# Six expert tiles moved into the end of the graph stage, and the first tile list made from the counts of 22 groups

## What is computed

```python
x = x + gnn(layernorm(x), adj, ...)        # agg = eps*x + adj @ x; silu(rmsnorm(agg @ W1 + b1)) @ W2 + b2
x = x + ffn(layernorm(x), ...)
# ffn:
topk_vals, topk_idx = top_k(x @ gate_w + gate_b, 2)
topk_w = softmax(topk_vals)
expert_out = relu(x @ w1[e] + b1[e]) @ w2[e] + b2[e]       # experts 16, hidden 256
y = x + sum(topk_w * expert_out at topk_idx)
out = (y - mean(y)) / sqrt(var(y) + 1e-5) * gamma + beta
```

## Time and profile before

| what | value |
|---|---|
| median of 3 runs | 845.04 us |
| the profiled execution's time | 846.69 us |
| its span, first to last instruction | 844.9 us |
| PE busy, weight loads | 737.2 us (87%), 570.2 us (67%) |
| DVE, ACT, POOL busy | 625.5, 528.4, 519.3 us |
| mean granted TensorE clock | 0.946 of full |

### The profile page before, as it was taken

One profiled execution on the slowest core, in us unless ns is written; L12 is line 12 of the kernel. 1 busy time (PEld: TensorE's weight loads), 2 busy tenths in 40 slices (PEclk: granted clock), 3 DMA queues, 4 the chain that ended last, 5 costly groups with the idle time before them and its releaser, 6 DMA issues. The chain is left out here.

```text
span 844.9 us, 18953 instructions
## 1 busy us (share of the span) xinstructions
PE 737.2 (87%) x4709; PEld 570.2 (67%) x4710; DVE 625.5 (74%) x2290; ACT 528.4 (63%) x1123; POOL 519.3 (61%) x540
## 2 busy tenths in 40 slices
PE   4899999999999999995289999999999999998700
PEld 3577777787787777874167777777777777776500
DVE  2589999999999998886657666567776776666664
ACT  2589999999999999985223333355545445444441
POOL 3004777776677777767540067767777773777774
PEclk9799999999999999998579999999999999999955
DMA  5365555555555553221465577778888887888632
GB/s 160 117 227 193 176 167 176 190 190 191 182 173 177 167 174 121 74 82 53 118 195 150 156 204 197 211 206 225 235 229 229 225 225 206 225 231 223 196 109 81
DMA packets 141531, 149.20 MB, mean 177 GB/s; under 512 B 18835, under 2 KB 113059, under 8 KB 141222
## 3 DMA queue, kind: packets, MB, share of 16 engines
q1 hardware_dynamic: 122614, 111.13, 43.5%
q0 software_dynamic: 16384, 34.11, 14.2%
q10 hardware_dynamic: 2480, 3.40, 1.3%
HBM read 83.02 MB, written 65.55 MB: 176 GB/s over the span
## 5 line engine op out<-in xcount | busy, mean ns | idle before, releaser
L482 POOL DMA_INDIRECT dispatched<-rows,slot_i x256 | 258.3, 1009 | 169.1 <-issue 160.7
L501 POOL DMA_INDIRECT work<-results,place x184 | 182.7, 993 | 118.7 <-DVE tout L1200 63.2
L817 ACT ACTIVATE hid<-bank,wts 128x256 f32<-128x256 f32 x286 | 119.9, 470 | 212.1 <-PE bank L681 210.2
L1200 DVE SCALAR_TENSOR_TENSOR tout<-bank,gate,tin 128x128 f32<-128x128 f32 x286 | 87.2, 346 | 119.3 <-PE bank L696 118.4
L696 PE MATMUL bank<-w_all,hid 128*128 x1144 | 165.9, 288 | 0.0
L681 PE MATMUL bank<-tut,wts 128*128 128x256 f32 x572 | 150.0, 386 | 6.9 <-DVE tut L1183 6.9
L696 PEld LDWEIGHTS bank<-w_all,hid 128*128 128x128 f32 x1144 | 138.7, 191 | 17.2 <-issue 0.2
L533 PEld LDWEIGHTS bank<-w_sb,work 128*128 128x128 f32 x1024 | 123.2, 194 | 17.6 <-issue 14.6
L533 PE MATMUL bank<-w_sb,work 128*128 128x128 f32 x1024 | 126.4, 278 | 1.6 <-ACT work L796 1.6
L527 PE MATMUL bank<-agg,w_sb 128*128 128x512 f32 x256 | 125.2, 612 | 0.0
L681 PEld LDWEIGHTS bank<-tut,wts 128*128 128x128 f32 x572 | 98.6, 193 | 16.4 <-DVE tut L1183 8.1
(11 more groups left out here) (186 smaller groups left out, 1049.3 us busy)
## 6 DMA issues: line engine op xcount, KB each, us to landing
tin<-dispatched SPq DMA_DIRECT2D x143, 132.0 KB
wts<-in_w_exp SPq DMA_DIRECT2D x143, 129.0 KB
results<-tout SPq DMA_DIRECT2D x26, 704.0 KB, 5.2
results<-tout SPq DMA_DIRECT2D x143, 128.0 KB
xs<-in_x SPq DMA_DIRECT2D x32, 256.0 KB, 3.3
adj_sb<-in_adj_t SPq DMA_DIRECT2D x32, 256.0 KB
rms_b<-r_row SPq DMA_DIRECT2D x32, 256.0 KB, 3.5
out<-agg SPq DMA_DIRECT2D x32, 256.0 KB
```

The source lines that it names most:

```text
L482: nc.gpsimd.indirect_dma_start(dispatched, bass.IndirectOffsetOnAxis(slot_i[:, k, n:n + 1], 0), rows[:, k, n // TOPK, n % TOPK, :], None). ...
L501: nc.gpsimd.indirect_dma_start(moe_of(g)[:, n // TOPK, n % TOPK, :], None, results, bass.IndirectOffsetOnAxis(place[:, g, n:n + 1], 0)).th ...
L817: last = nc.scalar.activation(hid[:, n % 2, c, :], hid_ps[n % 2][:, c * TILE:(c + 1) * TILE], ACT.Relu, bias=wts[:, k, F + c:F + c + 1], s ...
L1200: last = nc.vector.scalar_tensor_tensor(out=tout[:, k, a, :], in0=exp_ps[n % 2][:, a * D:(a + 1) * D], scalar=gate[:, n % 2, a:a + 1], in1 ...
```

## The change

The first six tiles (0 to 5) are no longer run behind the routing, but between its last steps, in an order that is written out by hand for PE, ACT and DVE: after step 32 come tile steps -1 and 0, after step 33 tile step 1, after step 34 tile step 2, and so on to tile step 5; the totals, the whole list and the pads go in between. For that their list has to exist earlier. It is now made from the counts of 22 groups (EARLY_AT), which PE sums in step 25 and DVE turns into the six entries in six parts, one at the end of each of steps 26 to 31. SyncE waits for the scatters of 22 groups instead of 29. The counts of all segments are still taken after step 31 (`tiles_by_then`, `lists_of_tiles`: the old block without the first list). FIRST is 10 (tiles behind it are loaded only when everything is scattered), which makes MIX_FROM 44. DVE's first wait for a stored tile moves from tile 3 to tile 6. Each engine's tile loop now starts behind tile step 5. SyncE's order of work is unchanged.

```diff
 RING2 = 6
 NT = TOK * TOPK // TILE + E - 1
 CAP_T = CAP // TILE
-FIRST = 9
+FIRST = 10
+EARLY_AT = 22
+EARLY_STEP = EARLY_AT + 3
 FULL_AT = 29
 SEGS = (2, 4, 6, 9, 12, 15, 18, 21, 25, FULL_AT)
...
-                sp.wait_ge(scattered[k], 16 * GB * TOPK * len(range(k, FULL_AT, RING)))
+                sp.wait_ge(scattered[k], 16 * GB * TOPK * len(range(k, EARLY_AT, RING)))
...
-            pipeline(eng, tile_step, -1, 7, NG // RING2, MIX_FROM, RING2)
+            pipeline(eng, tile_step, RING2, 2 * RING2 + 1, NG // RING2 - 1, MIX_FROM, RING2)
...
+                    if i is None and t == EARLY_STEP + 1:
+                        pe.wait_ge(early_out, 1)
...
+                if i is None and t == EARLY_STEP:
+                    pe.wait_ge(hist_done, EARLY_AT)
+                    for q, upto in enumerate((SEGS[0], EARLY_AT)):
+                        for j in range(GB):
+                            last = nc.tensor.matmul(q_ps[:, (4 + q) * E:(5 + q) * E], ones_b[:], hist[:, upto - 1, j, :],
+                                                    start=(j == 0), stop=(j == GB - 1))
+                    last.then_inc(early_done, 1)
...
-            pipeline(pe, step, *P1)
+            pipeline(pe, step, *P1[:3], NG)
...
+                    listed = first_table if i is None and n < RING2 else table
+                    e = pe.value_load(listed[0:1, bass.ds(count(i, n, 1, RING2), 1), 1], min_val=0,
...
+            step(None, NG)
             pe.wait_ge(x1_done, NG)
-            pe.wait_ge(table_done, 1)
+            pe.wait_ge(z_done, HC * NG)
+            pe.wait_ge(rb_out, NG)
+            pe.wait_ge(first_done, 1)
             pe.wait_ge(b2_in, 16)
             pe.wait_ge(w2_in, 16 * FC)
-            pipeline(pe, tile_step, *P2, RING2)
+            tile_step(None, -1)
+            tile_step(None, 0)
+            step(None, NG + 1)
+            tile_step(None, 1)
+            step(None, NG + 2)
+            tile_step(None, 2)
+            pe.wait_ge(carry_done, NG)
+            pe.wait_ge(slote_done, NG)
+            pe.wait_ge(ms_out, NG)
+            for j in range(GB):
+                last = nc.tensor.matmul(misc_ps[:, 0:E], ones_b[:], carry[:, NG % RING, j, :],
+                                        start=(j == 0), stop=(j == GB - 1))
+            last.then_inc(tot_done, 1)
+            tile_step(None, 3)
+            tile_step(None, 4)
+            pe.wait_ge(cols_done, 1)
+            for q in range(2):
+                nc.tensor.transpose(q_ps[0:1, q * (P + E):q * (P + E) + P], t_c[:, q, 0:1], ident[:])
+                last = nc.tensor.transpose(q_ps[0:1, q * (P + E) + P:(q + 1) * (P + E)], t_c[0:E, q, 1:2],
+                                           ident[0:E, 0:E])
+            last.then_inc(rows_done, 1)
+            pe.wait_ge(back_done, 1)
+            nc.tensor.transpose(misc_ps[0:1, 0:P], t_c[:, 2, 0:1], ident[:])
+            nc.tensor.transpose(misc_ps[0:1, P:P + E], t_c[0:E, 2, 1:2], ident[0:E, 0:E]).then_inc(rows_done, 1)
+            tile_step(None, 5)
+            pe.wait_ge(table_done, 1)
+            pipeline(pe, tile_step, RING2, P2[1], P2[2], P2[3], RING2)
...
-            pipeline(act, step, *P1)
+            pipeline(act, step, *P1[:3], NG)
...
+            step(None, NG)
+            tile_step(None, 0)
+            step(None, NG + 1)
+            tile_step(None, 1)
+            step(None, NG + 2)
+            for t in range(2, 5):
+                tile_step(None, t)
+            act.wait_ge(pad_done, 1)
+            _, starts = nc.values_load_multi_w_load_instructions(
+                pad_row[0:1, E // 2:E], engines=[mybir.EngineType.Activation], min_val=0, max_val=E * CAP)
+            for r in starts:
+                act.dma_start(pad_rows(r), pad[:]).then_inc(padded, 16)
+
+            tile_step(None, 5)
...
+            def early_tiles(part):
+                ceil, full = nt_ef[:, 0], nt_ef[:, 1]
+                if part == 0:
+                    link(nc.vector.tensor_scalar(nt_e[:, 0, 0], early_c[:, 0], float(TILE - 1), None, ALU.add))
+                    link(nc.vector.tensor_scalar(nt_e[:, 0, 1], early_c[:, 1], 0.0, None, ALU.add))
+                    link(nc.vector.tensor_single_scalar(nt_e[:, 1], nt_e[:, 0], TILE.bit_length() - 1,
+                                                        op=ALU.arith_shift_right))
+                    link(nc.vector.tensor_copy(nt_ef[:], nt_e[:, 1]))
+                if part == 1:
+                    link(nc.vector.tensor_tensor(pick[:, 0:E], full, ceil, ALU.min))
+                    link(nc.vector.tensor_tensor(pick[:, E:], full, pick[:, 0:E], ALU.subtract))
+                    link(nc.vector.tensor_copy(run2[:, 0, E:], pick[:]))
+                for step in {1: (0,), 2: (1, 2, 3, 4)}.get(part, ()):
+                    a, b = run2[:, step % 2], run2[:, (step + 1) % 2]
+                    link(nc.vector.tensor_tensor(b[:, E:], a[:, E:], a[:, E - (1 << step):3 * E - (1 << step)], ALU.add))
+                if part == 3:
+                    link(nc.vector.scalar_tensor_tensor(out=fill[:], in0=pick[:], scalar=float(FIRST),
+                                                        in1=run2[:, 1, E:], op0=ALU.add, op1=ALU.subtract))
+                    link(nc.vector.scalar_tensor_tensor(out=fill[:], in0=fill[:], scalar=0.0, in1=pick[:],
+                                                        op0=ALU.max, op1=ALU.min))
+                    link(nc.vector.tensor_tensor(upto_t[:, 1, :], fill[:, 0:E], fill[:, E:], ALU.add))
+                    link(nc.vector.tensor_copy(run[:, 0, NS - 1, E // 2:], upto_t[:, 1, :]))
+                if part == 4:
+                    running_sum(NS - 1, 1)
+                if part == 5:
+                    across = lambda a: a.unsqueeze(1).broadcast_to([1, RING2, E])
+                    link(nc.vector.tensor_scalar(away[:], upto_t[:, 1, :], -1.0, float(CAP_T), ALU.mult, ALU.add))
+                    link(nc.vector.tensor_tensor(f_m[:, 0], across(run[0:1, 0, NS - 1, E // 2:]),
+                                                 iota_ef[0:1, 0:RING2].unsqueeze(2).broadcast_to([1, RING2, E]),
+                                                 ALU.is_le))
+                    link(nc.vector.tensor_tensor(f_m[:, 1], f_m[:, 0], across(away[0:1, :]), ALU.mult))
+                    link(nc.vector.tensor_reduce(f_s[:], f_m[:], axis=AX.X, op=ALU.add))
+                    link(nc.vector.tensor_tensor(f_r[:], f_s[:, 1, :], iota_ef[0:1, 0:RING2], ALU.add))
+                    link(nc.vector.tensor_scalar(first_table[:, :, 0], f_r[:], float(TILE), None, ALU.mult))
+                    nc.vector.tensor_scalar(first_table[:, :, 1], f_s[:, 0, :], float(P), None, ALU.mult)\
+                        .then_inc(first_done, 1)
...
+                    if i is None and t == EARLY_STEP:
+                        dve.wait_ge(early_done, 1)
+                        nc.vector.tensor_copy(early_c[:], q_ps[:, 4 * E:6 * E].rearrange("p (q e) -> p q e", e=E))\
+                            .then_inc(early_out, 1)
-                if i is None and t == NG:
-                    first_tiles()
+                if i is None and EARLY_STEP < t < NG:
+                    early_tiles(t - EARLY_STEP - 1)
...
-                    if n >= LAG:
+                    if i is None and n == RING2:
+                        for k in range(RING2 - LAG):
+                            dve.wait_ge(t_kept[k], 16)
+                        k = n % RING2
+                    if n >= RING2:
...
-                if i is None and t == 0:
-                    late_tables()
...
+            step(None, NG)
+            tile_step(None, -1)
+            step(None, NG + 1)
+            tile_step(None, 0)
+            tiles_by_then()
+            tile_step(None, 1)
+            step(None, NG + 2)
+            tile_step(None, 2)
+            lists_of_tiles()
+            tile_step(None, 3)
+            totals()
+            tables()
+            dve.wait_ge(u_done, NG)
+            dve.wait_ge(slots_done, NG)
+            tile_step(None, 4)
+            places(None, 0)
+            tile_step(None, 5)
```

132 lines of the change are left out of this document (46 added, 86 removed).

## The result

The changed kernel takes 848.66 us (median of 20 executions) beside 845.07 us for the kernel before in the same session: ratio 1.0051, 95% interval 1.0036 to 1.0066. (One of the 20 executions of the kernel before took 1904.53 us; the median hardly feels it.) Forecast was 846.2 us; the range held the result. The sign came out as forecast and, in the main, the mechanism; the size did not: some 3.6 to 4.3 us instead of 1.2. The profiled execution took 851.05 us with a span of 849.2, 2.4 us above its kernel's median; that of the kernel before was 1.6 us above its own.

What follows compares the result with a forecast made beforehand. SyncE's queue was taken to bound the tiles, 2.59 us a turn, without rest from tile 8. Its load of tile 8 moves from 440.20 to 441.4 us, +1.2 us on the median 845.04: 846.2 us, range 840.5 to 850.0.

Steps and rivals of the forecast that it cites:

- The pace and the path to the end: Tile loop: SyncE's queue paces at 2.59 us a turn; its shift reaches the end through POOL's wait for tile 110.
- The totals at 426.0: On DVE, behind the tile steps and lists: totals begin at 426.0 us, not at 417.85.
- window for right: Sign that the forecast holds: the totals on DVE (copy of tot) begin at 426 +- 1.5 us.
- sign for wrong: Sign against the forecast: the totals on DVE begin before 423 or after 428.5 us.
- its hidden layer, still at full clock: PE's hidden layer of tile 0, first moved tile: 1.03 us at full clock, relu done at 400.3 us.
- second rival: Clock stays up in the two tile steps on the chain: 2.4 not 4.4 us each, 842.9 us; chance 0.18.
- The cost of the early counts and list: Steps 25 to 31 on PE and DVE: last group's sum ends at 397.0 us instead of 395.13.
- 9.24 + 0.9: Totals to the end of SyncE's pads 9.24 us, then register loading 0.9 us before the first store.
- Tile 8's load at 441.4: SyncE's queue: tile 8 loaded at 441.4 us against 440.20 before, +1.2 us, and the same at the end.
- PE's hole ahead of tile 6: PE idle 10 us or more before tile 6, which lands near 439.8 us.
- third rival: DVE hardly waits for the moved tiles: totals at 419.4 us, -5.4 us at the end, 839.6 us; chance 0.10.
- The cold restart: PE restarts at half clock for four tile steps from tile 6; queue waits 4.4 us, 850.6 us; chance 0.13.

Runs made afterwards that it cites:

- load_less: Kernel before, with weights from a fixed expert per buffer, so two registers instead of three read per SyncE turn; output differs; 832.52 us, ratio 0.9843.
- early_only2: Changed kernel's early list from 22 groups kept, the six tiles put back behind the graph stage, segment lists made after step 33; 840.09 us, ratio 0.9952.
- after_busy: Changed kernel with unneeded matmuls on PE, 6 ahead of the list's transposes and 9 behind them; 851.59 us (four executions), ratio 1.0076 to the kernel before.
- out_late2: Changed kernel with DVE's output of tile 0 moved behind the last group's routing; 845.93 us, ratio 1.0011 to the kernel before.
- the pairs: SyncE reads the list for two tiles in one register load; on the kernel before 844.03 us, with early list and tiles put back 836.09 us.

## Why the prediction was right, and where its size was off

**The pace and the path to the end: right.** "From about tile 25 on PE runs at SyncE's pace, and SyncE's queue is without rest from tile 8" is shown by load_less. That a head start reaches the end is shown by early_only2, in full in its trace and by half in its median. The Trainium skill's rule (Perfetto Trace Analysis, Identifying the Most-Contended Engine), weighed there, takes the busiest engine, PE, for the limit. By it load_less could have gained nothing; it gained 13 us.

**The totals at 426.0: 428.21.** This is outside the prediction's window for right (1.5 us either way) and 0.3 us short of its sign for wrong (after 428.5). Counted from the end of the last sum, the forecast was 29.0 us and the trace has 30.65 (397.56 to 428.21). It breaks at one term: "its hidden layer, still at full clock". It took 2.05 us, the half clock's time, behind gate matmuls at half clock (8 in 1.73 us). The prediction took the full clock without a row for it, and its argument against its second rival says the opposite, that PE "already at 390.88" ran at half clock. In the trace of before the granted clock was back at 0.90 from 394 to 396.5 us; in the changed kernel it was 0.50 from 394 to 400. With 0.4 us that tile 0's transposes came late behind those, and 0.6 us of the sum itself, the relu ended at 402.32 instead of 400.3. Everything behind it kept its forecast length: from there to the rows 2.1 us, to the logits on DVE 13.0 (forecast 13.0), to the totals 25.9 (25.7). The cost of the early counts and list, 1.9 us on the last sum, cannot be checked closely: the four profiles without them have it at 393.8 us on average (390.88 to 395.82), the six with them at 395.0 (393.62 to 396.87). That the changed kernel's sum ended within 0.6 us of the forecast 397.0 is therefore partly luck, and the 1.9 us, more than the whole forecast shift of 1.2, are neither shown nor refuted.

**From the totals to the first store: 9.24 + 0.9 forecast, 10.87 measured.** Two errors of opposite sign. SyncE issued its eight pads in 4.99 us and not 5.99, so the last column of the table, ready at 436.71, came last. And the store followed it by 2.37 us, not by 0.9. after_busy has 2.36 for the same step, out_late2 2.13. The price was taken from a turn in full run. Of the other 1.5 us, 1.1 are in the register load itself. The queue's register loads from the list, the first one alone and all 143, nearly all of them of three registers (ns: shortest, median, longest; us: first and last start):

```profile
L389 SPq TENSOR_LOAD <-table x1: 1745/1745/1745, 436.8 to 436.8; - x1
...
L389 SPq TENSOR_LOAD <-table x143: 273/672/1745, 436.8 to 803.1; - x143
```

The kernel before paid this too, 1.85 us at 427.8, but there the queue waited 3.9 us for tile 0's output anyway. Why the first load is slow stays open.

**Tile 8's load at 441.4: 444.46,** the sum of these: 2.2 + 1.5 less 0.7 for pads and table. So the two mis-sized terms are the clock of tile 0's hidden layer and the first turn of the queue. From there, turns and POOL as forecast; the queue's waits, 1.9 us in all, were near the forecast none. POOL's small wait behind the long one (1.76 us at 765.0) was there before as well (2.48 us at 761.2).

**PE's hole ahead of tile 6:** from 430.8 to 442.11 us with 1.4 us of list transposes in it, so 9.9 us idle; 10 or more were forecast.

**The rivals.** The clock did not stay up in the two steps on the chain (1.91 us for the hidden layers of tiles 1 and 2, at 410.54 and 418.79; tile 3's, at 422.88, took 1.03, too late to help). DVE did wait for the tiles, 3.29 and 3.03 us, the reason given against the third rival. The cold restart did not hold the queue here (0.6 us of waits for outputs): one tile step ran at half clock, not four, and the queue itself was late. In out_late2, with its lead back, it did.

## What to carry to other kernels

A queue that only issues transfers never shows as busy; look at its waits. If it has none and a busy engine waits for its loads now and then, the queue may set the pace. Here one register less in its turn gave 13 us (in a kernel that leaves out the choice of the expert), and the best reordering of the engines' work, with the pairs, 9.

Before work is put into a hole, ask what stands behind it on each in-order engine. Here six tiles that cost nothing on PE made DVE wait 6.3 us for two outputs, on the chain that made the list; placed behind the routing, one of them no longer did.

Here the hole, half filled, left the clock low on both sides: hidden layers of 2.05 and 1.91 us in it and 1.91 us behind it. Earliness won by a reordering can be lost in the half clock of the restart behind it, as in out_late2.

A trace is one execution. Where it is the fastest or slowest of its kernel, read the ratio of medians beside it.

## What the runs showed of the hardware that was not expected

- Reading three registers and getting to the next store takes SyncE 0.87 us, two 0.67 us, six 1.48 us, none 0.19: it goes with the registers. The register load alone takes 0.67, 0.47 and 1.28 us (medians for three, two and six), 0.2 us a register. Reading in pairs saves nothing in straight code.
- The first load of three registers from the list behind the waits and pads took 1.50 to 2.26 us in the four kernels with the six tiles moved (1.75 in the changed kernel), and the store followed the end of the list by 2.1 to 2.9 us.
- Matmuls that nobody needs hold the granted clock: after 8.34 us of them a hidden layer took 1.03 us; after 4.15 us of them and 2.03 us without, 1.92.
- One chip ran the same kernel 1.5 times as long (1264 us, mean granted clock 0.805), with ratios between kernels that agreed in sign where they told anything.
